# Products of zeros ahead of the first weights, and eight layer norms applied by ScalarE

## The reference

```python
x = x + _L0_xattn_ref(_layernorm(x, axis=-1), ctx_1024, ...)
x = x + _L0_attn_ref(_layernorm(x, axis=-1), ...)
x = x + _L0_ffn_ref(_layernorm(x, axis=-1), ...)
```

```python
def _layernorm(x, axis=-1, eps=1e-05):
    m = jnp.mean(x, axis=axis, keepdims=True)
    v = jnp.var(x, axis=axis, keepdims=True)
    return (x - m) / jnp.sqrt(v + eps)

def self_attn(x, Wq, Wk, Wv):
    Q, K, V = (x @ Wq, x @ Wk, x @ Wv)
    energy = jnp.einsum('bqd,bkd->bqk', Q, K)
    ...
```

## Time and profile before

| | us |
|---|---|
| median of three runs | 1004.72 (1004.12 to 1005.21) |
| profiled execution | 1003.91 |
| its span | 1002.2 |
| TensorE busy | 985.2 (98%) |
| VectorE busy | 615.4 (61%) |
| ScalarE busy | 393.6 (39%) |
| GpSimd busy | 216.4 (22%) |

### The profile page before, as it was taken

How to read it: one execution, slowest core, us unless ns; L and a number is a source line. 1 busy time by engine, 2 the same in 40 slices (tenths; PEclk the granted TensorE clock), 3 DMA queues, 4 the chain that set the end, 5 groups by cost and what they waited for, 6 DMA issues and landing times.

```text
span 1002.2 us, 14420 instructions
## 1 busy us (share of the span) xinstructions
PE 985.2 (98%) x5412; PEld 775.0 (77%) x5412; DVE 615.4 (61%) x1147; ACT 393.6 (39%) x631; POOL 216.4 (22%) x202
## 2 busy tenths in 40 slices
PE   8999999999999999999999999999999999999998
PEld 4886444445454458878888888999999999999997
DVE  6368543444656465896556667777656656656666
ACT  2332221222111144355576752544544445445441
POOL 2053400002000026464412124630000000000051
PEclk9999999999999999999999999999999999999999
DMA  9809699999999933033311100696674756645553
GB/s 295 318 1 375 245 361 417 405 417 394 411 391 416 384 108 85 1 85 98 113 48 37 32 11 8 235 295 197 209 199 145 202 167 198 182 155 183 154 149 133
DMA packets 45959, 206.91 MB, mean 206 GB/s; under 512 B 5760, under 2 KB 16256, under 8 KB 41680
## 3 DMA queue, kind: packets, MB, share of 16 engines
q1 hardware_dynamic: 40256, 187.95, 52.9%
q0 software_dynamic: 5648, 18.22, 5.5%
HBM read 190.04 MB, written 16.12 MB: 206 GB/s over the span
## 4 chain that ended last, share of the span: by engine, by line
PE 85%; DVE 7%; DMA 6%; issue 1%; ACT 0%; SPq 0%; POOL 0%; DVEq 0%; ACTq 0%
PE ps L486 59%; PE ps L621 7%; PE ps L650 7%; DMA big<-in_ctxT 3%; DMA big<-in_ctx 2%; DVE stats L1316 2%; PE ps L480 2%; PE ps L598 1%; PE ps L952 1%; PE ps L979 1%; PE ps L654 1%; PE ps L631 1%; PE ps L856 1%; PE ps L493 1%; PE ps L532 1%; DMA xr<-in_x 1%
## 5 line engine op out<-in xcount | busy, mean ns | idle before, releaser
L486 PE MATMUL ps<-x,w 128*128 128x320 f32 x1536 | 235.5, 309 | 0.0
L486 PEld LDWEIGHTS ps<-x,w 128*128 128x128 f32 x1536 | 228.0, 188 | 0.4
L1847 DVE TENSOR_TENSOR w<-big,w 128x1536 fp32r<-128x1536 f32 x64 | 112.1, 1753 | 78.3 <-ACT w L1250 78.3
L486 PE MATMUL ps<-hsplit,w 128*128 128x320 f32 x672 | 107.7, 309 | 0.0
L1250 ACT CAST w<-big 128x1536 fp32r<-128x1536 f32 x64 | 94.3, 1475 | 29.4 <-PE ps L486 26.9
L486 PEld LDWEIGHTS ps<-hsplit,w 128*128 128x128 f32 x672 | 100.8, 188 | 0.1
L486 PE MATMUL ps<-xcT,u 128*128 128x512 f32 x432 | 98.2, 389 | 0.0
L621 PE MATMUL ps<-big 128*64 128x512 f32 (+2 forms) x512 | 95.9, 500 | 1.6 <-DMA big<-in_ctxT 0.9
L486 PEld LDWEIGHTS ps<-xcT,u 128*128 128x128 f32 x432 | 81.0, 188 | 17.0 <-DVE xcT L1628 0.2
L650 PE MATMUL ps<-big 128*64 128x512 f32 x384 | 86.4, 597 | 2.0 <-DMA big<-in_ctx 1.9
L621 PEld LDWEIGHTS ps<-big 128*64 128x64 f32 x512 | 43.4, 136 | 53.1 <-issue 39.8
(11 more groups left out here) (338 smaller groups left out, 1542.9 us busy)
## 6 DMA issues: line engine op xcount, KB each, us to landing
big<-in_ctxT SPq DMA_DIRECT2D x16, 3202.0 KB, 18.8
big<-in_ctx SPq DMA_DIRECT2D x16, 3072.0 KB
big<-in_w_units SPq DMA_DIRECT2D x64, 768.0 KB, 4.5
big<-in_dense_units SPq DMA_DIRECT2D x41, 256.0 KB, 2.7
xs<-big POOLq DMA_DIRECT2D x1, 5120.0 KB, 17.4
big<-in_gate_units SPq DMA_DIRECT2D x12, 384.0 KB, 3.0
hr<-xs SPq DMA_DIRECT2D x28, 160.0 KB, 5.8
ys<-big POOLq DMA_DIRECT2D x28, 160.0 KB, 5.5
```

The source lines that it names most:

```text
L486: mm = nc.tensor.matmul(dst, lhs[x], rhs[w], start=start and x + w == 0, stop=stop and x == 1)
L1847: V.tensor_tensor(wsplit[f % RING][1][:], wraw[f % RING], wsplit[f % RING][0][:].bitcast(F32), ALU.subtract).then_inc(w_low, 1)
```

## The change

It does three things. TensorE multiplies the tile of zeros by itself three times (256 columns, into bank 7) before it waits for the first weights. ScalarE applies the eight first norms, as scale times x plus bias with two columns: the scale is the inverse deviation, the bias is minus mean times inverse deviation (`centre`, which shares the memory of `rsum`, used only later). VectorE computes this column (`first_centre`) where it applied the norm; the counter `ln_scaled` starts at 8 for its later users.

```diff
@@
+        centre = rsum
@@ TensorE
+            pe.wait_ge(zero_set, 1)
+            for k in range(3):
+                nc.tensor.matmul(ps[:, 7, 0:256], zeros[:, 0:P], zeros[:, 0:256], start=True, stop=True)
             for e in range(DC):
                 pe.wait_ge(wq1_in[e], 32)
@@ ScalarE
+            for i in range(NT):
+                act.wait_ge(ln_scaled, i + 1)
+                nc.scalar.activation(hr[:, i, :], xr[:, i, :], ACT.Identity, bias=centre[:, i:i + 1],
+                                     scale=rstd[:, i:i + 1]).then_inc(ln_norm[0], 1)
             for c in range(DC):
                 wait_filled(act, "m1", c)
                 nc.scalar.copy(m1[0][:, c, :], bank("m1", c)).then_inc(first_high, 1)
@@ VectorE
-            scaled = [0]
+            scaled = [NT]
+
+            def first_centre(i):
+
+                dve.wait_ge(ln_rstd[0], before[0] + i + 1)
+                V.scalar_tensor_tensor(centre[:, i:i + 1], mv[:, i, 0:1], -1.0, rstd[:, i:i + 1],
+                                       ALU.mult, ALU.mult).then_inc(ln_scaled, 1)
@@
                 norm_stats(0, i, xr[:, i, :])
                 if i:
-                    norm_apply(0, i - 1, xr[:, i - 1, :])
-            norm_apply(0, NT - 1, xr[:, NT - 1, :])
+                    first_centre(i - 1)
+            first_centre(NT - 1)
```

## The result

The changed kernel took 1005.28 us in the median of 20 runs (1002.96 to 1007.36), the kernel before 1003.73 us in as many (1002.20 to 1007.28). The ratio is 1.0016, with a 95% interval of 1.0009 to 1.0024: 1.6 us slower, within the 0.2% bound (the interval reaches just over it) and clear of zero. The profiled execution took 1006.18 us with a span of 1004.4, against 1003.91 and 1002.2 before, 2.3 and 2.2 us more.

The account below looks back on a forecast made before the run. The prediction took the front's chain of waits through GpSimd, VectorE's norms and low parts into gT as the bound, TensorE running unbroken after it. Zeros 0 plus norms 0.30 on 1004.72 gave 1005.0 us, range 1003.2 to 1006.4.

Parts of the forecast that it names:

- within 0.2%: Whole kernel: the measured time differs from the kernel before by no more than 2.0 us; chance 0.93.
- The chain to gT: Waits from the last norm to gT's products: ScalarE's norms delay m1high, so gT starts at 25.21, 0.30 us later.
- The terms inside it: Durations ahead of gT: activation 0.80 us, power 0.57, last column 0.17, eight VectorE low-part operations 4.87.
- The zeros: TensorE's start: zeros run from 1.5 to 4.1, the rate doubles sooner, m1 ends near 19.4, saving 1.4 us there.
- By itself this edit is worth 0: Products of zeros at TensorE's start: m1 isn't on the path, so they change the end by 0.
- rival 3: Ahead of gT: TensorE idles 2.1 us, its clock drops to 1.2 GHz, 2.5 us lost, 1007.5 us; chance 0.04.
- the 0.3 of the queue: ScalarE's queue: eight norms stand ahead of m1high, so gT's products start 0.30 us later.
- Rival 1: m1 at the start: the clock rises later in the runs, the kernel before pays 0.55 us, 1004.5 us; chance 0.20.
- Rival 2: ScalarE's norms: x lands about 1.4 us sooner, ScalarE comes free in time, gain 1.1 us, 1003.6 us; chance 0.10.
- Rival 4: TensorE's start: zeros leave the rate doubling at 9.4 or run past 4.37, 1005.0 to 1005.5 us; chance 0.02.

Follow-up runs that it names:

- six and two norms: The changed kernel with its last two norms back on VectorE, six on ScalarE, zeros at the start only: 1003.72 us (0.9996), again 1003.65 us (1.0000).
- six norms and filler: The changed kernel with its last two norms back on VectorE and three more products of zeros before the eighth tile's transposes: 1003.70 us, ratio 1.0002.

## Why the prediction was right or wrong, point by point

The measured 1005.28 us lies in the range, and the ratio of 1.0016 in the case "within 0.2%" that had 0.93. But that it lies only 0.3 us from the forecast 1005.0 is luck. The forecast was 1004.72 + 0.3; the kernel before took 1003.73, 1.0 us less than the three runs behind that number, and the change cost 1.55 us instead of 0.3. Two errors of about 1 us cancelled.

- **The chain to gT** was read rightly. ScalarE's norms stand ahead of m1high and take the place of VectorE's; the forecast was +0.30 us. The profile of the change has +0.89, of which 0.62 is the later landing of x; +0.27 is left. The norms alone start gT at 25.01, +0.10, with x landing 0.17 us earlier than before: +0.27; the whole change run again starts it at 25.25, +0.34, with x 0.07 us later: +0.27. In time they gave 0.9998 (0.9988 to 1.0008), which agrees and is too small to be seen.
- **The terms inside it.** The activation takes 0.813 us (0.80 taken), the power 0.55 (0.57), the last column 0.16 (0.17), and VectorE's eight low parts 2.48 + 2.40 (4.87). The row of the Trainium skill that the prediction cites ("ScalarE: Activation LUTs", section "Rules for kernel authors"), which sends add and mul to VectorE, was borne out for the last tiles (0.81 against 0.55 us): leaving two of them on VectorE took ScalarE off the path. For the first six it makes no difference, since ScalarE idles.
- **The zeros** run from 1.50 until the first real product at 4.28, and m1's rate doubles within its first round: 8 records in 4.45 us, those from 5.99 on 0.43 us apart (6.5 forecast). In this profile TensorE then waits 0.57 us for the second round's weights, which I hadn't priced, and m1 ends at 19.86. Over the eight profiles with zeros m1 ends between 18.80 and 19.86, over the four without between 20.25 and 21.16; so the forecast 19.4 and the gain of 1.4 us were right.
- **"By itself this edit is worth 0" is the step that failed.** The argument was that m1 isn't on the path, and in the chain of waits it isn't. But an engine that comes early to a wait is idle for longer, and here that costs: alone, this edit is 1.0012 (1.0002 to 1.0022), 1.3 us in the medians, with gT's 96 products at 23.61 us instead of 22.01. The term that the sum puts at nothing is the rate of gT behind the gap; the idle time itself was worked out, under rival 3.
- **Rival 3 was the usual case, with a chance of 0.04.** Its mechanism, its place and its gap (2.1 us worked out, 1.87 found) were right. Its price was 2.5 us: I took the slow stretch to be as long as at the start, 5 us. It was 3.4 us in the profiles (26.3 to 29.7 above) and cost 1.6 us. And it came in 22 of 31 executions. So 0.7 x 1.6 = 1.1 us, with the 0.3 of the queue 1.4 us, against 1.6 measured (1.61 between the means of the 20 runs each). The chance was mis-sized because the one row that spoke against it, full rate after 0.87 us, is from a gap half as long.
- **Rival 1** (the rise of the clock differs so that the kernel before pays) had a true premise, but its price isn't seen. The rise does differ from run to run, which no run could show yet when the prediction was written: without zeros the slow records of m1 number 5 to 7 in the four profiles, and m1 ends at 20.25 to 21.16. That is at most 0.3 us behind the kernel before's 20.84, where the rival wanted 0.75; and zeros with the gap filled give 0.9999 (0.9987 to 1.0010), no gain. **Rival 2** didn't occur: the earliest landing in any profile, 15.03, is 0.65 us sooner and not 1.4. **Rival 4** fell: the zeros do what they say.

## What to carry to other kernels

Before making TensorE faster or earlier at a place that isn't on the path, ask what it does with the time: if it then stands idle ahead of a dense stretch, that stretch may start at the lower clock, and the price is read from the records behind the longest gap, not from the chain. A cheap test is to fill the gap with products into a free bank; if the time falls although work was added, suspect the clock, and look whether the granted clock of the stretch behind the gap has risen too. And when moving work to an idle engine, leave the last instance where the next consumer's queue isn't behind it: six of eight norms could move for nothing, the last two put ScalarE on the path, for 0.3 us in the chains of waits (in the times that is too little to be seen).

## What the runs showed of the hardware that I had not expected

- After 1.81 to 1.87 us of idle time on TensorE the granted clock fell to 0.50 in all four profiles with such a gap; in the eight profiles with a gap of 1.03 us or less ahead of the same products (among them 0.58, 0.49, 1.03 and 0.34 us) it stayed at 1.00. It isn't shown that the idle time alone decides: ahead of it TensorE did only transposes since the end of m1, and that whole lighter stretch, too, was longer where the clock fell (5.3 to 6.1 us from the end of m1 to gT, against 4.0 to 4.5 in the unfilled profiles without a fall). The fall needn't come at once: in two of the four the first products still ran at 2.4 GHz, for 1.2 us in one of them. The windows of the second profile of six and two norms:

```profile
22.00:23.00 1.00, 0.29 (x3) 0.05 (x1) 1.00 (x3) 0.90 (x2) 0.00 (x0) 1.00 1.04 403
23.00:24.00 1.00, 0.00 (x0) 0.00 (x0) 0.85 (x2) 0.97 (x3) 0.00 (x0) 1.00 1.05 399
24.00:25.00 1.00, 0.90 (x4) 0.80 (x5) 0.01 (x1) 1.00 (x3) 0.00 (x0) 1.00 1.06 389
25.00:26.00 1.00, 1.00 (x5) 0.83 (x4) 1.00 (x2) 1.00 (x3) 0.00 (x0) 0.70 1.04 387
26.00:27.00 1.00, 1.00 (x4) 0.71 (x4) 1.00 (x3) 0.43 (x1) 0.00 (x0) 0.50 1.31 494
```

- Whether it falls differs between executions of one kernel: 22 of 31 of the change, 5 of 11 of the zeros alone, 3 of 23 of the version with six and two norms. In the four profiles with a fall, m1's records came to stand 0.43 us apart at 4.95 to 5.99 us, and the fall came 20.2 to 20.3 us after that, at 25.1 to 26.3. Whether the moment of the rise has a part in the fall no run here tests.
- The granted clock read 1.00 at the start of the program although records of 0.85 us and more in the earlier trace rows say 1.2 GHz. For the first products the durations tell the level and the column doesn't.
- GpSimd's power took 0.55 us beside VectorE's statistics and column operations, and 0.81 us (17.83 to 18.64 in the run with six norms and filler) once VectorE's apply of 512 columns, from 17.69 to 18.24, ran beside it again. The Trainium skill, "SBUF — State Buffer", section "Who interferes with whom", says that VectorE and GpSimd share a pair of ports, that `tensor_scalar` (the apply is one) can run in a mode that needs the pair, and that whichever of the two engines issues first then keeps it for its whole instruction. The trace fits: the apply started first and the power took longer; which mode the apply ran in no view says. This gives back 0.26 us of what the last two norms on VectorE gain.
